# Output projection inside the last attention batch, and the second normalisation with one root and two tiles a bank

## The reference

```python
x = x + tanh(g_xattn) * attention(layernorm(x), ctx, ctx, group_prob, mask)   # ends with out @ wo + bo
x = x + tanh(g_ffn) * ffn(layernorm(x))
# attention: softmax(q k / 4 + mask) * group_prob, times v, by head
# layernorm: (x - mean) / sqrt(var + 1e-5)
# ffn: normed = h * rsqrt(mean(h*h) + 1e-8) * norm_weight
#      shared = relu(normed @ sw1 + sb1) @ sw2 + sb2
#      routed = the two experts with the highest sigmoid(normed @ router.T), weighted
#      ffn = shared + routed
```

## Time and profile before

| | us |
|---|---|
| median of three runs | 666.57 |
| lowest, highest | 665.66, 667.86 |
| the profiled execution, time | 669.29 |
| its span | 667.5 |
| TensorE busy | 585.5 (88%) |
| VectorE busy | 436.9 (65%) |
| ScalarE busy | 428.9 (64%) |
| GpSimd busy | 295.5 (44%) |
| mean granted clock of TensorE, share of full | 0.942 |

### The profile page before, as it was taken

The page is one execution under the profiler, slowest core; times in us unless marked ns, Lnnn a source line. Parts: engine busy times, 40 slices in busy tenths (PEclk is TensorE's granted clock), DMA queues, the critical chain, the costliest instruction groups (busy, mean ns, idle before and its releaser), DMA issues.

```text
span 667.5 us, 18976 instructions
## 1 busy us (share of the span) xinstructions
PE 585.5 (88%) x6006; PEld 492.4 (74%) x6006; DVE 436.9 (65%) x1190; ACT 428.9 (64%) x1072; POOL 295.5 (44%) x329
## 2 busy tenths in 40 slices
PE   2779999999999999999766996699999999999950
PEld 2448888888888888887545884488888888888840
DVE  5857888888888888888685752145554535445327
ACT  4367888888888888888726561256565746656330
POOL 8303444444444444446540077242476545567120
PEclk9898999999999999999985898699999999999995
DMA  8725556785556566632050042112645743452228
GB/s 231 179 66 126 164 145 178 200 212 144 140 150 146 148 153 150 152 91 72 1 188 3 1 137 102 48 51 45 172 123 146 182 119 111 116 170 62 49 68 309
DMA packets 106776, 84.28 MB, mean 126 GB/s; under 512 B 42915, under 2 KB 100517, under 8 KB 106606
## 3 DMA queue, kind: packets, MB, share of 16 engines
q1 hardware_dynamic: 103694, 75.59, 43.3%
q0 software_dynamic: 3040, 8.16, 3.4%
HBM read 50.45 MB, written 28.30 MB: 118 GB/s over the span
## 4 chain that ended last, share of the span: by engine, by line
PE 60%; issue 8%; DVE 7%; ACT 6%; POOL 4%; DMA 4%; SPq 2%; POOLq 1%; ACTq 0%; DVEq 0%
PE ps L1137 15%; PE ps L1124 14%; PE ps L981 10%; PE ps L999 5%; PE ps L898 5%; PE ps L968 5%; PE ps L929 3%; ACT probs L763 2%; POOL w L628 2%; ACT ctxT L687 2%; POOL w L626 1%; DMA kst<-k_scratch 1%; DVE probs L1286 1%; PE ps L1112 1%; DMA words_in<-x_sent 1%
## 5 line engine op out<-in xcount | busy, mean ns | idle before, releaser
L981 PE MATMUL ps<-ident,probs 112*125 112x112 f32 x768 | 193.2, 278 | 1.8 <-DVE arena L1298 0.7
L763 ACT ACTIVATE probs<-probs,negmax 112x375 f32<-112x375 f32 x256 | 154.5, 607 | 12.6 <-DVE negmax L1286 12.1
L981 PEld LDWEIGHTS ps<-ident,probs 112*125 112x125 f32 x768 | 139.4, 188 | 23.7 <-issue 9.4
L816 ACT ACTIVATE arena<-ps,b 128x256 f32<-128x256 f32 x192 | 79.3, 463 | 119.9 <-PE ps L1124 104.4
L1137 PE MATMUL ps<-w,arena 128*128 128x256 f16 x1152 | 135.4, 276 | 12.7 <-issue 10.7
L1286 DVE CUSTOM_DVE_ANT_0 probs<-ps,neg 112x375 f32<-112x375 f32 x256 | 136.9, 540 | 5.0 <-issue 1.3
L1137 PEld LDWEIGHTS ps<-w,arena 128*128 128x128 f16 x1152 | 112.9, 99 | 31.4 <-issue 17.3
L1431 DVE TENSOR_TENSOR arena<-arena 128x512 f16<-128x512 f32 x96 | 74.6, 784 | 93.4 <-ACT arena L821 82.4
L1298 DVE TENSOR_TENSOR arena<-ps,gpT 125x336 f32<-125x336 f32 x192 | 97.1, 506 | 41.2 <-PE ps L981 37.5
L553 POOL TENSOR_TENSOR probs<-probs,gp_in 112x375 f32<-112x375 f32 x64 | 58.6, 916 | 147.9 <-ACT probs L763 147.6
L1124 PE MATMUL ps<-probs,w 128*128 x816 | 92.0, 273 | 1.1 <-DMA probs<-x_sent 0.6
(11 more groups left out here) (170 smaller groups left out, 792.4 us busy)
## 6 DMA issues: line engine op xcount, KB each, us to landing
kst<-k_scratch SPq DMA_DIRECT2D x64, 140.6 KB, 3.7
w1s<-in_L_ffn_ew_dram SPq DMA_DIRECT2D x8, 1024.0 KB
w2s<-in_L_ffn_ew_dram SPq DMA_DIRECT2D x8, 1024.0 KB, 5.6
x_sent<-y_sb SPq DMA_DIRECT2D x12, 516.0 KB, 5.9
ctx_in<-in_ctx_dram SPq DMA_DIRECT2D x16, 375.0 KB
k_scratch<-kT SPq DMA_DIRECT2D x32, 187.5 KB, 2.5
arena<-y_back SPq DMA_DIRECT2D x7, 512.0 KB, 6.9
k_scratch<-kT SPq DMA_DIRECT2D x32, 93.8 KB, 2.1
```

Source lines behind the costliest of these rows:

```text
L763: act.activation(probs[:, n % PROBS], probs[:, n % PROBS], ACT.Exp, bias=negmax[:, p, n:n + 1], scale=-1.0, accum_out=rowsum[:, p, ORDER[n ...
L816: act.activation(hid32[:, f], ps[:, f // 2 % 4, f % 2 * TILE:(f % 2 + 1) * TILE], ACT.Relu, bias=b1[:, f, e:e + 1]).then_inc(h_relu, 1)
L981: mm = pe.transpose(ps[0:KP, PT[n % 2], c * S:(c + 1) * S], probs[:, n % PROBS, c * KP:(c + 1) * KP], ident[0:S, 0:S])
```

## The change

**Projection.** In the last batch TensorE projects two tiles behind each of the heads 11 to 15, ten tiles, and the last four behind the batch. It uses three banks (4, 6, 7), so it waits for a take only from tile 3 on. VectorE takes two tiles in the same head slots, makes the statistics of the tile before and the mean of the one before that. The row sums of the last batch are inverted behind head 13 and transposed behind head 15 into a bank of the scores.

**Normalisation.** ScalarE centres (mean minus x, so the sign is turned), GpSimd multiplies by the norm weight, and the last batch's `split_out` stands on GpSimd behind the product of tile 7. The root is taken of a quarter of the former argument, which saves the step by one half, and comes out negative, which turns the sign back. ScalarE loads its table for the square root right behind the last exponential.

**Pairs.** ScalarE scales the even tiles, VectorE the odd ones, VectorE makes both low halves. TensorE transposes two tiles into one whole bank, ScalarE copies a bank by one instruction of 1024 columns. TensorE makes the first two columns of the first hidden tile before it multiplies the last two tiles by the router; the ranks come after the whole hidden tile.

**Moved.** The bias is added in batches 1 to 4 instead of the last two. The shared expert's weights are split by GpSimd alone, in eight pieces, in batches 11 to 13; these are written out and no longer in the loop.

```diff
+DOUBLES = NT // 2
+PJ_FROM = 11
...
-        xn2 = arena[:, 0:NT * D].rearrange("p (i d) -> p i d", i=NT)
+        ARENA, XN2 = H // 2 * T // 2, H // 2 * T // 2 - 9 * D
+        assert XN2 >= QW + AT * KC * S and (NT - 9) * D <= QW
+        xn2 = [arena[:, at:at + D] for at in ((XN2 + i * D) % ARENA for i in range(NT))]
...
+        PJ = (4, 6, 7)
...
+                    if isinstance(t, int) and 1 <= t <= QC and k in (0, 2):
+                        add_out_bias(2 * (t - 1) + k // 2)
+                    if isinstance(t, int) and t > QC and k != 1:
+                        split_shared((t - SPLIT_FROM) * 3 + (k + 1) // 2)
...
+                pool.tensor_copy(high, of).then_inc(sw_hi, 1)
+                pool.wait_ge(sw_hi, n + 1)
+                pool.tensor_tensor(low, of, high, ALU.subtract).then_inc(sw_lo, 1)
...
-            split_out(B - 1)
-
-
-            pool.wait_ge(w1_hi, 1)
-            pool.tensor_tensor(w1[:, 0, LO], w1s[:, :, :], w1[:, 0, HI], ALU.subtract).then_inc(w1_lo, 1)
-            pool.wait_ge(w2_hi, 1)
-            pool.tensor_tensor(w2[:, 0, LO], w2s[:, :, :], w2[:, 0, HI], ALU.subtract).then_inc(w2_lo, 1)
...
+            for i in range(NT):
+                if i == 2 * (H - PJ_FROM) - 2:
+                    split_out(B - 1)
+                pool.wait_ge(n2_centered, i + 1)
+                pool.tensor_tensor(xn2[i], xn2[i], nw_bc[:, :], ALU.mult).then_inc(n2_made, 1)
...
-            take_sums(B - 1, 1)
-
-
-            act.wait_ge(in_w1, 16)
-            act.activation(w1[:, 0, HI], w1s[:, :, :], ACT.Copy).then_inc(w1_hi, 1)
-            act.wait_ge(in_w2, 16)
-            act.activation(w2[:, 0, HI], w2s[:, :, :], ACT.Copy).then_inc(w2_hi, 1)
+
+            def center(tiles):
+                for i in tiles:
+                    act.wait_ge(x2_mean, i + 1)
+                    act.activation(xn2[i], x_sb[:, i], ACT.Identity, bias=mv[:, i, 0:1], scale=-1.0).then_inc(n2_centered, 1)
+
+            def normal_high(i):
+                act.wait_ge(n2_made, i + 1)
+                act.activation(xpair[:, i, 0:D], xn2[i], ACT.Copy, scale=nrm[:, 2, i:i + 1]).then_inc(n2_hi[0], 1)
+
+            def turned(j):
+                act.wait_ge(n2_T, 2 * j + 2)
+                act.activation(x2T[:, :, :, 2 * j * P:2 * (j + 1) * P].rearrange("p a c t -> p (a c) t"),
+                               ps[:, j % 4].bitcast(F16).rearrange("p (c t) -> p c t", t=2 * P), ACT.Copy).then_inc(n2_Ts, 1)
+
+            act.activation(nrm[:, 5, FIRST], nrm[:, 2, FIRST], ACT.Sqrt)
+            center(range(2 * (H - PJ_FROM) - 4))
+            take_sums(B - 1, SC[0])
+            center(range(2 * (H - PJ_FROM) - 4, NT - 1))
             act.wait_ge(dve_ask, 3)
             act.activation(nrm[:, 1], nrm[:, 0], ACT.Sqrt).then_inc(act_gave, 1)
-            def turned(i):
-                act.wait_ge(n2_T, i + 1)
-                act.activation(x2T[:, :, :, i * P:(i + 1) * P].rearrange("p a c t -> p (a c) t"),
-                               ps[:, i % 4, 0:D].bitcast(F16).rearrange("p (c t) -> p c t", t=P), ACT.Copy).then_inc(n2_Ts, 1)
-
+            center(range(NT - 1, NT))
             act.wait_ge(root_made, 1)
-            for i in range(NT):
-                act.wait_ge(n2_made, i + 1)
-                act.activation(xpair[:, i, 0:D], xn2[:, i], ACT.Copy, scale=nrm[:, 2, i:i + 1]).then_inc(n2_hi, 1)
-                if i >= 2:
-                    turned(i - 2)
-            turned(NT - 2)
-            turned(NT - 1)
+            for j in range(DOUBLES):
+                normal_high(2 * j)
+                if j >= 1:
+                    turned(j - 1)
+            turned(DOUBLES - 1)
...
+            def project(i):
+                made = -(-(i + 1) * P // S)
+                pe.wait_ge(oT_hi, made)
+                pe.wait_ge(oT_lo, made)
+                if i == 0:
+                    pe.wait_ge(prep_act, 7 * B + 1)
+                    pe.wait_ge(o_read, B - 1 + O_FREE)
+                if i >= 3:
+                    pe.wait_ge(x2_made, i - 2)
+                parts = [(a, w, k) for k in range(ND) for a, w in PASSES]
+                for j, (a, w, k) in enumerate(parts):
+                    mm = pe.matmul(bank(PJ[i % 3], P, D), oT[:, a, k, i * P:(i + 1) * P], wpair[:, 3, w, k],
+                                   start=(j == 0), stop=(j == len(parts) - 1))
+                mm.then_inc(pj_mm, 1)
...
+                    if not t_next and n >= PJ_FROM:
+                        if n == H - 1:
+                            pe.wait_ge(sc_read, H * B + SC_FREE)
+                            turn_sums(t, SC[0])
+                        for i in range(2 * (n - PJ_FROM), 2 * (n - PJ_FROM) + 2):
+                            project(i)
...
+            for i in range(2 * (H - PJ_FROM), NT):
+                project(i)
...
+            def turn_normal(i):
+                pe.wait_ge(n2_hi[i % 2], i // 2 + 1)
                 pe.wait_ge(n2_lo, i + 1)
-                if i >= 4:
-                    pe.wait_ge(n2_Ts, i - 3)
+                if i >= 8 and i % 2 == 0:
+                    pe.wait_ge(n2_Ts, i // 2 - 3)
+                to = ps[:, i // 2 % 4].bitcast(F16).rearrange("p (c t) -> p c t", t=2 * P)
                 for c in range(2 * ND):
-                    mm = pe.transpose(ps[:, i % 4, 0:D].bitcast(F16)[:, c * P:(c + 1) * P], xpair[:, i, c * P:(c + 1) * P], ident16[:, :])
+                    mm = pe.transpose(to[:, c, i % 2 * P:(i % 2 + 1) * P], xpair[:, i, c * P:(c + 1) * P], ident16[:, :])
                 mm.then_inc(n2_T, 1)
...
+            for i in range(NT):
+                turn_normal(i)
+                if i % 2 == 1 and i > 1:
+                    route(i - 3)
+                    route(i - 2)
+            pe.wait_ge(w1_lo, 1)
+            hidden(0, shared_rows(0), range(2))
+            route(NT - 2)
+            route(NT - 1)
+            hidden(0, shared_rows(0), range(2, NF))
...
+            def tile_stats(i):
+                dve.wait_ge(x2_made, i + 1)
+                dve.bn_stats(stats[:, i], x_sb[:, i]).then_inc(x2_stats, 1)
+
+            def tile_mean(i):
+                dve.wait_ge(x2_stats, i + 1)
+                dve.bn_aggr(mv[:, i], stats[:, i]).then_inc(x2_mean, 1)
+
+            def take_projection(i):
+                dve.wait_ge(pj_mm, i + 1)
+                if i == 0:
+                    dve.wait_ge(resid, -(-NT // BIAS_TILES))
+                dve.scalar_tensor_tensor(x_sb[:, i], bank(PJ[i % 3], P, D), gates[:, 0:1], x_sb[:, i], ALU.mult, ALU.add).then_inc(x2_made, 1)
+                if i >= 1:
+                    tile_stats(i - 1)
+                if i >= 2:
+                    tile_mean(i - 2)
...
+                    if not prep and n >= PJ_FROM:
+                        for i in range(2 * (n - PJ_FROM), 2 * (n - PJ_FROM) + 2):
+                            take_projection(i)
+                        if n == H - 3:
+                            invert_sums(t, p)
...
-            invert_sums(B - 1, 1)
             divide(B - 1, 1)
 
 
-            for i in range(NT):
-                dve.wait_ge(pj_mm, i + 1)
-                if i == 0:
-                    dve.wait_ge(resid, -(-NT // BIAS_TILES))
-                dve.scalar_tensor_tensor(x_sb[:, i], bank(OB[i % 2], P, D), gates[:, 0:1], x_sb[:, i], ALU.mult, ALU.add).then_inc(x2_made, 1)
-                if i >= 1:
-                    dve.wait_ge(x2_made, i)
-                    dve.bn_stats(stats[:, i - 1], x_sb[:, i - 1])
-            dve.wait_ge(x2_made, NT)
-            then(dve.bn_stats(stats[:, NT - 1], x_sb[:, NT - 1]))
-            for i in range(NT):
-                last = dve.bn_aggr(mv[:, i], stats[:, i])
-            then(last)
-
-            then(dve.tensor_scalar(nrm[:, 4], mv[:, :, 1], LN_EPS, RMS_EPS, ALU.add, ALU.mult))
-            dve.tensor_tensor(nrm[:, 0], nrm[:, 4], mv[:, :, 1], ALU.add).then_inc(dve_ask, 1)
-
-            def center(tiles):
-
-                for i in tiles:
-                    dve.scalar_tensor_tensor(xn2[:, i], x_sb[:, i], mv[:, i, 0:1], nw_bc[:, :], ALU.subtract, ALU.mult).then_inc(n2_made, 1)
-
-            center(range(2))
-            inverse_root(4, slice(0, NT))
-            dve.sem_inc(root_made, 1)
-            center(range(2, NT))
-            for i in range(NT):
-                dve.wait_ge(n2_hi, i + 1)
-                dve.scalar_tensor_tensor(xpair[:, i, D:2 * D], xn2[:, i], nrm[:, 2, i:i + 1], xpair[:, i, 0:D],
+            def negative_root():
+
+                dve.wait_ge(x2_mean, NT)
+                then(dve.tensor_scalar(nrm[:, 4], mv[:, :, 1], LN_EPS, 0.25 * RMS_EPS, ALU.add, ALU.mult))
+                dve.scalar_tensor_tensor(nrm[:, 0], mv[:, :, 1], 0.25, nrm[:, 4], ALU.mult, ALU.add).then_inc(dve_ask, 1)
+                dve.wait_ge(act_gave, 4)
+                then(dve.reciprocal(nrm[:, 3], nrm[:, 1]))
+                then(dve.tensor_tensor(nrm[:, 3], nrm[:, 3], nrm[:, 0], ALU.mult))
```

(23 more changed lines are left out.)

96 lines of the change are left out of this document (52 added, 44 removed).

## The result

The changed kernel took 661.19 us in the median (659.04 to 664.3) against 667.94 us (665.66 to 670.81) of the kernel before, measured beside it: 6.75 us faster. The ratio is 0.9889 with its interval [0.987, 0.9908]; the two medians alone give 0.9899. The forecast was 9.4 us. The profiled execution of after took 662.9 us with a span of 661.1, 6.4 less than before.

What follows compares the result with a forecast made beforehand. VectorE was taken to bound the seam between attention and shared tiles from 333 to 354 us; 11.1 us gained at the first result matmul less 1.7 for the clock gave 9.4, so 666.6 - 9.4 = 657.2 us, range 652 to 662.5.

Steps and rivals of the forecast that it cites:

- part 5: Weight splits and bias additions moved over GpSimd in earlier batches: taken as 0, hidden by its idling; upper bound 1.2 us.
- part 1: Projection inside the last batch: VectorE's variances ready at 341.0 instead of 346.5, with 1.25 us of waits on TensorE.
- the walk: Slot-by-slot count of VectorE's waits in the last heads: 0.45 at tile 2, 0.5 at tile 4, 0.3 at tile 13.
- part 2: The root after the means: a chain of 1.6 us, ending at 342.6 instead of 348.8; first transpose at 343.6.
- The rival's mechanism: VectorE's projection takes and GpSimd's products exclude each other in the new tail: 9.4 us on top, no change; chance 0.04.
- the core of part 2: Centring, 4.84 us for twelve tiles on VectorE, goes to ScalarE and GpSimd and is hidden there.
- part 3: Pairs of normalised tiles a bank: 1.42 us a pair, hidden matmuls starting 9.8 us after the first transpose, at 353.4.
- part 4: New wait for VectorE's routing behind the first hidden tile: TensorE idles 2.0 us, results start at 363.4 instead of 374.51.
- Clock: 1.7 forecast: TensorE's 2.0 us idle before the results brings a half-clock stretch costing 1.7 us; rival without clock loss, 655.5, chance 0.25.
- the 11.1 us: Gain forecast at the first result matmul, 363.4 instead of 374.51, before the clock's price of 1.7 us.
- neither rival: TensorE's stall during the scatter grows, up to 15 us more (chance 0.06), or goes, 15 us less (chance 0.08).
- the prediction's last sign of being wrong: A gain at the first result matmul that the end of the shared tiles doesn't keep.

Runs made afterwards that it cites:

- e1: Changed kernel with the last batch's split moved on GpSimd from behind the product of tile 7 to behind tile 4's: 642.58 us beside 650.17 of before, 0.9892.
- e6: Changed kernel with two GpSimd products before the row sums' spread, last split behind tile 6's product, ScalarE's scalings one pair further ahead: 657.81 us, 0.9847.
- e8: Changed kernel with all 14 projections and takes put back behind the last batch: 660.95 us, 0.9894.
- e2: Changed kernel with GpSimd's last three products held back until the root is made: 642.89 us, 0.9886.
- e11: Changed kernel with centring and norm-weight product back on VectorE in one operation a tile: 645.1 us, 0.9933.
- e3: Changed kernel with ScalarE's scalings of even tiles one pair further ahead of its copies: 639.56 us, 0.9868.
- e7: Changed kernel with 24 extra discarded matmuls on TensorE between the first hidden tile and the ranks: 661.55 us, 0.9915.
- e10: e6 and e7 together, on the changed kernel: 637.17 us beside 649.55 of before, 0.9808.
- e12: Changed kernel with at most four scatter transfers under way at a time: 642.1 us, 0.9879.
- e5: The changed kernel again, unedited, beside the kernel before on the same chip: 662.38 us against 667.45, 0.9915.

## Why the prediction was right, and where its steps were off

The sign, the place and the range were right; the forecast was 2.7 us too good. Little of that cancels: 2.2 us were missing up to the first result matmul and 1.6 in the stall, against 0.4 that the clock cost less. The steps, against the profile:

**Attention and the moved GpSimd work (part 5): right.** The takes start at 326.44, for the forecast's 326.3. Since the first take moves by up to 2.9 us between traces of the same attention, the batches say more: 11 to 13, with the eight weight pieces, take 17.5 to 17.9 us from split to split on GpSimd, the others 17.57.

**Means (part 1): the waits were mis-sized.** Forecast 341.0, measured 341.5. I had the split's end at 338.4 and a wait of 0.3; it was 339.1 and 1.48. I had let GpSimd follow ScalarE's centrings, but in its order the spread of the sums stands ahead of all products, and that came at 332.1; e1 and e6 show the wait go to nothing. The other waits of VectorE were smaller than the walk had them (0.37 at tile 4, hardly any at tile 2). In the sum part 1 held. But the claim behind it, that the interleaving is a large part of the gain, is not borne out: e8 puts it at 1 us at the root, 2.5 with the split early.

**Root (part 2): 1.6 forecast, 2.6 measured** (341.48 to 344.08). The missing 1.0 is the lock. I had dismissed it, as a rival, because the takes read PSUM. That is so, and the takes were not slowed; I didn't ask the same of the root's own steps and the differences, which have two SBUF inputs and lie beside the products too. e2 shows both. The rival's mechanism was thus real, at a tenth of its 9.4 us.

**Centring moved (the core of part 2): right in kind, over-rated in size.** e11 returns 4.3 us between root and first transpose, near the 4.84 I used, but gives 2.1 back by doing away with the products' side effects: net 2 to 3.

**Pairs (part 3): 1.42 forecast, 1.55 measured,** 0.8 in sum. I took the slowest engine's sum for the period. The copy was right (1.02 against 1.01), ScalarE and TensorE had time left, and still two pairs cost 3.1, because of a ring over three engines. e3 opens it.

**First hidden matmuls to results (part 4): 10.0 forecast, 9.7 measured,** but made up otherwise: the hidden matmuls end 6.8 us after their start instead of 8.0, with the full clock back at 358, and TensorE then idles twice, 1.84 us before the ranks and 0.75 before the results, where 2.0 in all were named.

**Clock: 1.7 forecast, 1.3 measured,** and shown by e7 and e10. It isn't certain in each case: of the eleven profiled kernels of this form without the added matmuls nine ran the first results at half clock at the start; e3, with the same 1.84 and 0.75 us of idle, and e12, with 0.94 and 0.75, did not. Why e3 didn't stays open.

So at the first result matmul 2.2 of the 11.1 us were missing: 0.5 the means, 1.0 the root, 0.2 the hand-overs, 0.8 the pairs, less 0.3. The clock gave 0.4 back. That makes 7.66 at the end of these results.

**The stall: neither rival, but not neutral.** It came again and stood in the same relation to the scatter: it begins 21.6 us after the first transfer (376.71), before 23.0 (384.35), and ends some 3 us behind the last. It took 1.6 us more than before, and so 6.0 to 6.3 of the 7.66 are left behind it and 6.4 at the end; on the chips without it 6.8 and 7.5 were measured, and 5.1 in e5 with it. That answers the prediction's last sign of being wrong: the end of the shared tiles does not keep all of the gain at the first result matmul, 8.95, of which the clock takes 1.3 and the stall 1.6. During it VectorE and ScalarE are nearly idle as well, while GpSimd's issues run on at their 1.27 us; no releaser is named. That it goes with the chip is seen in the times of the kernel before (650 and 667 us) and, for the changed kernel, in the traces of its variants; neither kernel was traced unedited on a chip without the stall. Its cause is open; the experiment on it was made twice and both times met a chip without it.

The change gains because the second normalisation begins earlier. That is not one part's merit. Undone alone, the interleaving is worth nothing in time and 1 us at the root, the pairs 0, the centring 2 to 3 us; together with the rest (one root step less, the hidden columns ahead of the last routings, the weight splits out of the way) they give 7. The rest was never undone, so that more than half of the gain is not told apart by these runs.

## What to carry to other kernels

When work is moved to an idle engine, write down that engine's queue in order, and look for the small instruction that others wait for; here the split of the last batch stood behind eight products, and moving two of these into an idle gap ahead of it, with one scaling more in flight, was worth 4.6 us. A period is the longest ring of hand-overs, not the busiest engine's sum: where the starts alternate (1.31, 1.78), an engine is waiting for its own earlier work. And undo each part of a change alone before believing what it brings: two of three here brought nothing alone.

## What was not expected of the hardware

- The lock between VectorE and GpSimd is felt most by tiny instructions: 14 columns with two SBUF inputs took 0.60 to 0.71 us beside GpSimd's product of 256 columns (0.69 a tile), and 0.17 alone.
- Discarded matmuls that bridge 2.6 us of idle are worth up to 1.5 us (5.40 against 6.97 for the 48 behind them). The clock doesn't fall behind every such gap: in two traces of eleven without them it stayed up.
- Chips differ by 17 us in 667 on the same kernel. A stall of TensorE, VectorE and ScalarE during 28 indirect transfers, some 15 us too long by the earlier trace rows, is in every trace taken on the slower ones and in none on the others.
- Two copies of 512 columns of float16 from PSUM by ScalarE cost 1.08 to 1.23 us, one of 1024 costs 1.02.
